# Attention with rotary position: the exchanged halves of q from a second projection, or from row transfers of a copy

## The reference

```python
q = (x @ Wq).reshape(Bd, Sd, H, DH + D_ROPE)          # H = 16, DH = 16, D_ROPE = 64
q_nope, q_rope = (q[..., :DH], q[..., DH:])
c_kv = x @ Wdkv
kv = (c_kv @ Wukv).reshape(Bd, Sd, H, 2 * DH)
k_rope = x @ Wkr
q_rope = q_rope * cos + rotate_half(q_rope) * sin     # rotate_half: (-x2, x1) of the halves x1, x2
scores = einsum(q_nope, k_nope) + einsum(q_rope, k_rope)
attn = softmax(where(causal, scores * scale, -1e9))
out = einsum(attn, v) @ Wo
```

## Time and profile before

| | |
|---|---|
| median of three runs | 1651.57 us |
| the profiled execution | 1649.07 us, of which 1647.3 us are the span of the profile |
| layer norm and weight split | about 11 to 39 us |
| attention | about 39 to 445 us; its loop of heads about 66 to 427 us |
| busy over the whole span | PE 79%, VectorE 63%, ScalarE 37%, GpSimd 38% |
| an instruction of 128 x 512 float32 | L738 0.68 us (VectorE), L803 1.27 (GpSimd), L655 0.63 (ScalarE) |

### The profile page before, as it was taken

One profiled execution on the slowest core, in us unless ns is written; L12 is line 12 of the kernel. 1 busy time (PEld: TensorE's weight loads), 2 busy tenths in 40 slices (PEclk: granted clock), 3 DMA queues, 4 the chain that ended last, 5 costly groups with the idle time before them and its releaser, 6 DMA issues. The chain is left out here.

```text
span 1647.3 us, 38818 instructions
## 1 busy us (share of the span) xinstructions
PE 1304.3 (79%) x13740; PEld 998.9 (61%) x13741; DVE 1044.2 (63%) x2169; ACT 609.4 (37%) x1320; POOL 629.9 (38%) x564
## 2 busy tenths in 40 slices
PE   2798998988548999993456868989898539999992
PEld 1355666665427999892223436666666528989981
DVE  6488898888673555555685656666666464555554
ACT  2456666766523333331355711111111113333330
POOL 0345454545202333320003257666667212333320
PEclk9899999999758999997678869999999759999996
DMA  4556666574357111113100000000000257111115
GB/s 139 141 154 171 168 167 176 151 178 138 111 176 298 48 46 46 51 39 116 50 1 13 0 14 2 2 2 2 2 3 2 78 176 288 49 51 45 48 36 166
DMA packets 98816, 145.95 MB, mean 89 GB/s; under 512 B 32961, under 2 KB 76738, under 8 KB 96386
## 3 DMA queue, kind: packets, MB, share of 16 engines
q1 hardware_dynamic: 87746, 118.00, 23.9%
q0 software_dynamic: 8832, 24.13, 4.8%
q10 hardware_dynamic: 2112, 2.10, 0.4%
HBM read 87.57 MB, written 39.32 MB: 77 GB/s over the span
## 5 line engine op out<-in xcount | busy, mean ns | idle before, releaser
L1162 ACT ACTIVATE ffn_h<-ffn_bank,ffn_b 128x256 f32<-128x256 f32 x368 | 154.6, 471 | 323.0 <-PE ffn_bank L114 270.6
L1318 DVE CAST ffn_hh<-ffn_h 128x512 f16<-128x512 f32 x184 | 81.7, 444 | 204.5 <-ACT ffn_h L1162 198.5
L993 POOL DMA_INDIRECT ffn_xs<-xn_rows,ffn_from_rows x92 | 91.6, 995 | 306.8 <-PE ffn_bank L1070 200.8
L2113 POOL TENSOR_TENSOR ssm_GL<-ssm_L,ssml_G 128x512 f32<-128x512 f32 x128 | 164.1, 1292 | 110.3 <-DVE ssm_L L2026 110.2
L112 PE MATMUL ffn_bank<-ffn_hh,ffn_W 128*128 128x256 f16 x736 | 200.6, 273 | 3.8 <-DVE ffn_hl L1320 3.8
L113 PE MATMUL ffn_bank<-ffn_hl,ffn_W 128*128 128x256 f16 x736 | 200.6, 273 | 0.0
L114 PE MATMUL ffn_bank<-ffn_hh,ffn_W 128*128 128x256 f16 x736 | 200.6, 273 | 0.0
L2026 DVE TENSOR_TENSOR_SCAN ssm_L<-ssm_bank,ssmh_ident 128x512 f32<-128x512 f32 x128 | 151.2, 1209 | 2.3 <-PE ssm_bank L1895 2.2
L1912 PE MATMUL ssm_Y<-ssm_GL,ssmh_windows 64*32 64x64 f32 x4096 | 143.2, 221 | 8.4 <-POOL ssm_GL L2113 8.0
L1000 POOL DMA_INDIRECT y_rows<-ffn_y,ffn_to_rows x92 | 91.1, 990 | 143.1 <-DVE ffn_y L1328 129.1
L1912 PEld LDWEIGHTS ssm_Y<-ssm_GL,ssmh_windows 64*32 64x32 f32 x4096 | 122.5, 109 | 36.7 <-issue 24.5
(11 more groups left out here) (340 smaller groups left out, 3248.3 us busy)
## 6 DMA issues: line engine op xcount, KB each, us to landing
ffn_W<-split_w SPq DMA_DIRECT2D x16, 2048.0 KB, 13.7
att_piece<-in_ffn_w SPq DMA_DIRECT2D x32, 512.0 KB, 5.2
split_w<-att_halves SPq DMA_DIRECT2D x32, 512.0 KB, 4.4
att_Q<-att_pair SPq DMA_DIRECT2D x64, 128.0 KB, 2.4
ffn_back<-y_rows SPq DMA_DIRECT2D x16, 512.0 KB, 5.1
att_KB<-att_krl SPq DMA_DIRECT2D x8, 512.0 KB, 5.3
att_Q<-att_pair SPq DMA_DIRECT2D x64, 64.0 KB, 2.0
xn_rows<-ffn_XN SPq DMA_DIRECT2D x8, 512.0 KB, 3.0
```

Source lines behind the costliest of these rows:

```text
L1162: ins_ = act.activation(h[layer][:, m, :], bank[1 + 2 * layer + u][:, (m % 2) * ST:(m % 2 + 1) * ST], ACT.Gelu, bias=bias[:, ds(e + m, 1)])
L2113: pool.tensor_tensor(GL[:, p % RING, :, :, :].rearrange("p x i n -> p x (i n)"), L[:, p % RING, :, :, :].rearrange("p x i n -> p x (i n)") ...
```

## The change

The second projection of a pair and its weights `wt` are gone. ScalarE copies the first bank into `turned[:, r % 2, 1, :]` (L643 of the new program). SyncE sends this copy in four transfers of 32 rows to a new tile `swapped`, with the halves exchanged (L401). VectorE makes the cosine product from the copy, no longer from the bank. GpSimd multiplies `swapped` with `sinT` (L825) and then adds (L833). `swapped` has two slots, by pair. The key's rotary part stays as it was. The host no longer builds `att_turned`. The diff, cut to its core:

```diff
@@ attention_stage, SyncE
+            def swap_rows(pr):
+
+                sp.wait_ge(swap_ready, pr + 1)
+                r = turn["pair", pr]
+                for x in range(4):
+                    rows, others = (slice(y * DR // 2, (y + 1) * DR // 2) for y in (x, x ^ 1))
+                    sp.dma_start(swapped[rows, pr % 2, :], turned[others, r % 2, 1, :]).then_inc(swap_in[pr % 2], 16)
...
             get_nope(("qn", 0), 0)
+            swap_rows(0)
             get_keys(0, 0)
             get_nope(("kn", 0), 0)
+            swap_rows(1)
             assemble(0)
...
                 if g % 2 == 0 and g >= 2 and g // 2 + 1 < NPR:
                     assemble(g // 2 + 1)
+                if g % 2 == 0 and g // 2 + 2 < NPR:
+                    swap_rows(g // 2 + 2)
@@ PE
                 if nth[job]:
                     pe.wait_ge(first_drained, nth[job])
+                    if done[nth[job] - 1][0] == "pair":
+                        pe.wait_ge(swap_ready, done[nth[job] - 1][1] + 1)
...
-                if job is None or job[0] == "lat":
+                if job is None or job[0] in ("lat", "pair"):
                     return
...
-                if what == "pair":
-                    ins = project(bank[1][:, :], wth, wtl, n % (NH // 2) * P, P, n // (NH // 2))
-                elif what == "kr":
+                if what == "kr":
@@ ScalarE, high_half
+                if what == "pair" and x == 0:
+                    r = turn[job]
+                    act.wait_ge(first_ready, nth[job] + 1)
+                    if r >= 2:
+                        act.wait_ge(summed, r - 1)
+                    act.activation(turned[:, r % 2, 1, :], bank[0][:, :], ACT.Copy).then_inc(swap_ready, 1)
+                    return
@@ VectorE, drain
+                    if what == "pair":
+                        dve.wait_ge(swap_ready, n + 1)
...
-                        ins = dve.tensor_tensor(to, bank[x][:, :], table[:, :], ALU.mult)
+                        ins = dve.tensor_tensor(to, turned[:, r % 2, 1, :], cosT[:, :], ALU.mult)
@@ GpSimd, sum_rope
+                if what == "pair":
+                    wait_alone(pool, swap_in[n % 2], 64 * (n // 2 + 1), passed)
+                    pool.tensor_tensor(swapped[:, n % 2, :], swapped[:, n % 2, :], sinT[:, :], ALU.mult).then_inc(sin_done, 1)
+                    wait_alone(pool, sin_done, n + 1, passed)
                 wait_alone(pool, first_drained, nth[job] + 1, passed)
-                wait_alone(pool, second_drained, nth_second[job] + 1, passed)
+                if what == "kr":
+                    wait_alone(pool, second_drained, nth_second[job] + 1, passed)
...
+                if what == "pair":
+                    pool.tensor_tensor(rope[:, r % 2, :], turned[:, r % 2, 0, :], swapped[:, n % 2, :], ALU.add).then_inc(summed, 1)
+                    return
@@ attention_layer
-            (rows(ins["att_turned"][0]), *wr), (rows(ins["att_turned"][1]), *wt), (rows(ins["att_mixed"]), *wx),
+            (rows(ins["att_rope"]), *wr), (rows(ins["att_mixed"]), *wx),
```

More of the change, by code:

```diff
@@ L274, in attention_stage @@
 def attention_stage(nc, X, XTh, XTl, weights, identf, identb, upper_neg, cosT, sinT, ffn_w, split_w, nope, xn_rows):
-    (wrh, wrl), (wth, wtl), (wxh, wxl), (wuh, wul), (woh, wol) = weights
+    (wrh, wrl), (wxh, wxl), (wuh, wul), (woh, wol) = weights
     QN_AT, LAT_AT, KR_AT, KT_AT = 0, NH * DH, NH * DH + LAT, NH * DH + LAT + P
@@ L285, in attention_stage @@
         turned, rope = t.sb("turned", [P, 2, 2, S]), t.sb("rope", [P, 2, S])
+        swapped = t.sb("swapped", [P, 2, S])
         pair = t.sb("pair", [P, 2, 2, S], F16)
@@ L305, in attention_stage @@
         moved = [sem(f"moved{i}") for i in range(2)]
+        swap_ready, swap_in = sem("swap_ready"), [sem(f"swap_in{i}") for i in range(2)]
+        sin_done = sem("sin_done")
         lat_high, qn_high, kn_high, v_high, oT_high = (sem(n) for n in ("lat_high", "qn_high", "kn_high", "v_high", "oT_high"))
@@ L333, in attention_stage @@
         nth = {job: n for n, job in enumerate(done)}
-        nth_second = {job: n for n, job in enumerate(j for j in done if j[0] != "lat")}
+        nth_second = {job: n for n, job in enumerate(j for j in done if j[0] not in ("lat", "pair"))}
         turn = {job: n for n, job in enumerate(j for j in done if j[0] in ("pair", "kr"))}
@@ L722, in drain @@
                 what, n = job
-                if what == "lat" and x:
+                if what in ("lat", "pair") and x:
                     return
                 if what in ("pair", "kr", "op"):
-                    if x == 0:
+                    if what == "pair":
+                        dve.wait_ge(swap_ready, n + 1)
+                    elif x == 0:
                         dve.wait_ge(first_ready, nth[job] + 1)
@@ L2182, in attention_layer @@
         XTh, XTl = pair("XT", [P, KD, B * S])
-        wr, wt, wx = pair("wr", [P, KD, NH * DR]), pair("wt", [P, KD, NH * DR]), pair("wx", [P, KD, NH * DH + LAT + 4 * DR])
+        wr, wx = pair("wr", [P, KD, NH * DR]), pair("wx", [P, KD, NH * DH + LAT + 4 * DR])
         wu, wo = pair("wu", [LAT, NH * 2 * DH]), pair("wo", [P, KD, D])
@@ L2186, in attention_layer @@
         parts = [
-            (rows(ins["att_turned"][0]), *wr), (rows(ins["att_turned"][1]), *wt), (rows(ins["att_mixed"]), *wx),
+            (rows(ins["att_rope"]), *wr), (rows(ins["att_mixed"]), *wx),
             (ins["att_up"], *wu), (rows(ins["L0_attn_a_Wo"]), *wo)]
         layer_norm_stage(nc, "ln0", X, None, XTh, XTl, c["identf"], lambda t: SplitWeights(t, parts))
-        attention_stage(nc, X, XTh, XTl, (wr, wt, wx, wu, wo), c["identf"], identb, upper_neg, cosT, sinT, ffn_w,
+        attention_stage(nc, X, XTh, XTl, (wr, wx, wu, wo), c["identf"], identb, upper_neg, cosT, sinT, ffn_w,
                         split_w, nope, xn_rows)
@@ L2230, in attention_weights @@
     swap = lambda w: np.concatenate([w[..., HALF:], w[..., :HALF]], axis=-1)
-    turned = np.stack([rope.reshape(D, NH * DR), swap(rope).reshape(D, NH * DR)])
     mixed = np.concatenate([nope, Wdkv, Wkr, Wkr, swap(Wkr), swap(Wkr)], axis=1)
     up = Wukv.reshape(LAT, NH, 2, DH).transpose(0, 2, 1, 3).reshape(LAT, 2 * NH * DH)
-    return {"att_turned": turned, "att_mixed": mixed, "att_up": up}
+    return {"att_rope": rope.reshape(D, NH * DR), "att_mixed": mixed, "att_up": up}
 def expert_pieces(W1, W2, W3):
```

## The result

The changed kernel took 1679.01 us (median of 4 runs, 1672.25 to 1679.78); the kernel before took 1652.3 us beside it (4 runs, 1646.07 to 1661.72). The medians differ by 26.7 us (1.6%). 1667 was forecast, 15.4 us up.

A forecast was written before the change was run, and what follows sets the result against it. The loop was taken as a chain of latencies. Layer norm -2.3, loop +1.5, start +5.2, batch changes +4 and clock +7 summed to +15.4 us on the median 1651.57: 1667 us, range 1642 to 1700.

The forecast's parts named there:

- What bounds the kernel: Attention loop: a chain of latencies, not PE or VectorE busy time; removed work is worth little unless on it.
- The new chain: Loop pairs: copy, four transfers, GpSimd product and sum give 10.93 us against 10.99; with jobs +0.15; loop +1.5 us.
- Batch changes: Three places where GpSimd runs without a pause: the extra 1.27 us product lies on the path, +4 us.
- Layer norm: Layer norm stage: the split of `wt` goes, with its 2.28 us VectorE subtraction, -2.3 us.
- The start: First two pairs, turned serially before the first scores: first exponential about 73.3 instead of 68.11, +5.2 us.
- Rival (b): Loop: transfers come late, or PE's clock falls in most pairs; one microsecond on 30 pairs gives +45, 1697; chance 0.22.
- The clock: Loop: PE idles longer, so its clock falls in 6 of 12 pairs instead of 2, 1.8 us each, +7 us.
- Rival (c): Loop: transfers quicker than the nearest rows, 10.6 us per pair, total 1645; chance 0.14 together with PE as the bound.
- Rival (e): Pairs with jobs: VectorE held by GpSimd's new instructions, up to 18 us more, 1685; chance 0.06.

The follow-up runs named there:

- run 4: Changed kernel without the row transfers (GpSimd multiplies the copy itself), VectorE's cosine product reading the projection's PSUM bank: 1640.39 us, 0.9922 of the kernel before.
- run 2: Kernel before with one matmul of the six in each pair's second projection: 1642.01 us, ratio 0.9909.
- run 5: Changed kernel with the second 512 KB transfer of the keys issued at head 5 of the batch, not head 3: 1675.76 us, 1.0113 of the kernel before.
- run 1: Changed kernel with the second projection's six matmuls back on PE from pair 2 on, result read by nobody: 1680.76 us, 1.0151 of the kernel before.
- run 12: Changed kernel with only the cosine product and the normalisation reading one operand from PSUM: 1683.06 us, 1.0166 of the kernel before.
- run 3: Changed kernel without the four row transfers, GpSimd multiplying the copy itself, halves not exchanged: 1659.81 us, 1.0041 of the kernel before.
- run 7: Changed kernel with a pair's high half (ScalarE's copy of GpSimd's sum) issued one head later: 1694.64 us, 1.0268 of the kernel before.
- run 10: Kernel before with a pair's high half one head later and the normalisation reading one operand from PSUM: 1644.22 us, ratio 0.9935.
- run 6: Changed kernel with, at the start, pair 1's copy ahead of pair 0's high half and its transfers ahead of the first key load: 1674.44 us, ratio 1.0123.

## Why the prediction was right, and where it missed

- **The number.** The measured median, 1679.0, lies 1 us above the forecast's own range (1660 to 1678) and inside the outer one (1642 to 1700). The direction is right, the rise came out larger: 26.7 us by the medians, about 21 by the ratio on record. (15.4 us are 0.93% of 1651.57, not 0.95.)
- **What bounds the kernel: right.** A loop of latencies. The removed PE and VectorE work was replaced on the path by copy, transfers and GpSimd's product. Run 4 shows what the same removal gives when they are absent (0.9922). Runs 2 and 4 add what I had not priced, where the next limit is: 10.5 us with a shorter sine path, 9.28 with VectorE's sine product gone too. So the new chain had 0.5 to 1.7 us per pair to lose.
- **The new chain: right in order, 0.2 us short.** Outside head 3, copy, issue and landing came as worked out (3.54 us, 591 ns, 2.0 us). The gap between two GpSimd instructions of which one waits for the other is 0.37 us; my 0.18 came from a cast and a subtraction. The twelve pairs that nothing disturbs rose by 2.8 us in sum, 0.23 each, where 1.5 was forecast for all 30.
- **Batch changes: right for the pair itself**, 4.0 against 4. That PE's wait for Q in the next pair would go (-1.7 us) was not foreseen.
- **Layer norm: mis-sized**, -1.3 instead of -2.3 (KA at 53.31 against 54.57). I read the removed instruction and not the blocks around it. In the new order the split of `wo` (0.67 us) moved from the last block, which ends on another engine, to one that VectorE ends, and the stage's first block started 0.2 us later:

```profile
29.00 0.67 DVE L146 TENSOR_TENSOR attw_wul<-ln_staged,attw_wuh 64x512 f16<-64x512 f32 x1
29.60 0.67 DVE L146 TENSOR_TENSOR attw_wol<-ln_staged,attw_woh 128x512 f16<-128x512 f32 x1
```

- **The start: mis-sized.** The first exponential came at 72.45, not 71: 1.0 of the 1.4 us is the layer norm, the rest the longer chain (8.05 us from one high half to the next, where 7.9 was worked out). By T2 another 1.2 us were gone.
- **Head 3: missed, and the largest error (+9.2).** I costed each of the four new issues in the chain, and not what they do to SyncE's queue behind them. "The four stand ahead of the store and load of their own pair" was true, but `assemble` stands behind store, load and keys. Rival (b), late transfers, held in these four pairs: what stood ahead of them on the queue was the burst of the head before. Run 5 took 7.6 of the 9.2 us back.
- **The clock: right in kind, and its sum near by luck.** I took four more pairs at 1.8 us. There were ten falls more (13 against 3), and the seven pairs in which nothing else happened had a mean of 12.46 us against 11.35 for the twelve without a fall: 1.1 us each. Their +6.1 us contain 1.6 of the longer chain. Whether a fall causes that 1.1 us or goes with a pair that stood still longer is not shown: with cover (run 1) half of the falls went and only 1.5 us with them.
- **Rival (c), quicker transfers:** landing 2.0, so it fell. **Rival (e), VectorE held:** the normalisation rose from 321 to 446 ns mean, but undoing it (run 12) shortened the loop by 4.8 us at most. The rival was nearer than its 0.06 says, not here but one edit away: in runs 3 and 7 it was the largest cost.
- **Range and chances.** Of the 10.6 us by which the loop rose more than forecast (26.0 against 15.4), 9.2 are head 3, 2.7 the stretch up to T2, 1.3 the chain; the pairs behind a batch change (-1.7) and the term of the clock (-0.9) work against them. The unforeseen gain hides part of what was missed.

## What to carry to other kernels

Price a new transfer twice: in its own chain, and for everything behind it on its queue, above all where that queue meets large transfers at fixed places. Before moving an instruction to hide a wait, look at what its successors on other engines will then stand beside; a wait can be what keeps GpSimd's SBUF reads apart from VectorE's instructions with two SBUF inputs, and giving those one PSUM operand makes the move pay (0.9935 instead of 1.0124). The kernel before with the PSUM operand and without the move was not run, so how the gain of run 10 divides between the two is open. Work taken off an engine at 89% returned half of its length in a pair (run 2), more where VectorE's product went with it (run 4: 11.02 to 9.28 us for 1.98 us of work), and nothing where a longer latency took its place.

## What the runs showed of the hardware

- VectorE's product of two SBUF tiles of 128x512 took 0.68 us alone, a median of 1.74 and at most 2.57 us beside GpSimd's; with one operand in PSUM 0.68 (0.69 at most) beside the same work. The normalisation of 128x64 went from 0.21 to 2.2 us at worst. I had expected it for one instruction in the jobs' pairs, not as the cost that decides on where GpSimd's work may stand.
- Row transfers between SBUF tiles of 64 KB each landed 1.9 to 2.6 us after their issue in the 64 of 128 cases whose landing is known. Behind the keys and the 512 KB pieces of head 3 they were later: the instruction that they released started 3.2 to 3.9 us after the last issue, against 2.2 elsewhere and 2.1 in the same pairs of run 5.
- The granted clock fell to 0.50 fourteen times in the changed kernel's loop, 8, 11 and 12 times in runs 5, 6 and 12, whose PE work is the same, and twice in run 2, which has less of it and shorter pairs. How often it falls was thus not told by PE's work; what decides it stays open.
